# Four layer normalisations of a decoder kernel move from VectorE to ScalarE

## The chip, the cores and the metric

The kernel runs on one core of one Trainium2 chip. The metric is the device time of one launch in microseconds (us). The engines are TensorE (PE, with its weight loads shown apart as PEld), VectorE (DVE), ScalarE (ACT), GpSimd (POOL) and SyncE (SP), which issues the DMAs. All work is float32 but for a few constant matrices in bfloat16.

## The reference, cut to what matters

A two-layer post-norm decoder over 16 sequences of 128 tokens with 256 features. Each of the six sublayers ends in a plain normalisation (no gain, no bias):

```
x = norm(x + L0_attention(x))          # 16 heads, rotary, latent heads
x = norm(x + L0_cross(ctx, x))         # linear attention, own gain and bias inside
x = norm(x + L0_ffn(x))                # gate/up 704 wide, FP4 quantise-dequantise
x = norm(x + L1_attention(x))          # causal, with a moving-average part
x = norm(x + L1_cross(x, ctx))         # softmax attention, MLP 1024, own gains
x = norm(x + L1_ffn(x))                # FP6 quantise-dequantise
norm(y) = (y - mean(y)) / sqrt(var(y) + 1e-5)
```

## The kernel before, in words

One tile is one sequence: 128 tokens on the partitions, 256 features along them. Every engine runs a list of *stages* (`l0_out`, `f0_norm`, `x1_project`, ...) for 16 tiles. Tiles overlap: a new one starts every `START` step, and at any time work of five or six tiles is interleaved. The order of the stages is fixed per engine before the program is built: `in_order` (L132) sorts all (stage, tile) pairs by `START[tile] + SLOTS[engine][stage]`. So a slot number says only where a stage stands in its engine's own queue, and a stage that has to wait holds up all stages behind it on that engine. Data that belong to a tile lie in one of four buffers (`b = tile % 4`).

A sublayer ends like this. PE fills a PSUM bank; DVE adds the residual and stores `y_` (`residual`, L1014), and takes the moments with two instructions, BATCH_NORM_STATS2 and BATCH_NORM_AGGREGATE (`moments`, L1008: `stats`, then `mean_var`). POOL (`root`, L654) adds eps (`var_eps`) and raises to the power -0.5 (`rstd`). Then one engine has to make `x_ = (y_ - mean) * rstd`, 128x256. Before the change that is DVE for all six norms, in `center` (L1028): one TENSOR_SCALAR with two per-partition operands. Behind it wait, depending on the norm: a transpose on PE (`l1_turn_x`, `x0_turn_x`, `x1_turn_x`, L1579), a bias addition on POOL (`bias`, L642), a copy into `v_` on ACT (L861), a shifted copy by DMA (L595) or the store of the output (L622).

The names that the prediction uses, with their engines: `f0_down` (PE, then the residual on DVE) ends the first FFN; `f0_norm` its norm; `l1_turn_x` transposes the result on PE, ACT copies it out of PSUM into `xt_`, `l1_project` (PE) uses it, ACT evicts the projections (L867, L826) and makes the tanh keys `l1_ka` (L877), after which PE may start `l1_scores`. `l0_out`/`l0_norm` belong to the next tile's first attention, `l1_out`/`l1_norm` to the second attention, `f1_out`/`f1_norm` to the last sublayer. `f0_quant`, `f0_scale`, `f0_level` (DVE, L963 to L1169) quantise `x_`; POOL dequantises (L695) into `k_`, and PE transposes that in `f0_turn_x`. `x0_kv` is a projection on PE that needs the PSUM bank which the second group of exponentials (`l1_exp1`, ACT, L793) has to empty first; DVE gives the exponentials their offset in `low` (L1073) after a maximum (`peak`, L1068).

In steady state the queues around the norms read as follows (tile numbers relative, t the tile in its FFN):

```
DVE: f0_down(t) x1_norm(t-2) l0_back(t+1) f0_norm(t) f1_quant(t-2) l0_out(t+1) l0_norm(t+1) f1_scale(t-2) f1_level(t-2) x0_mix(t+1)
     ... l0_rope(t+2) f1_out(t-2) x0_norm(t+1) l1_back(t) f0_quant(t+1) f1_norm(t-2) l1_below(t) ... f0_scale(t+1) f0_level(t+1)
     ... l1_out(t) l0_peaks(t+2) l1_norm(t) f0_gate(t+1)
```

Of the kernel before, what the change touches and what calls it, by code (L numbers as in the profile page):

```python
# [87 lines left out]
        round_up2=75562, quant_down0=75911, l0_inv=76161, quant_down1=76187, l0_back=76275, round_down0=76280,  # L88
        l0_out=76309, round_down1=76325, l0_norm=76329, x0_mix=76505, quant_last=76662, round_last=76861,
        x0_attend=76881, x0_affine=77034, x0_norm=77121, f0_quant=77139, f0_scale=77266, f0_level=77351,  # L90
        wo_bias=77798, x1_mask=77829, f0_gate=78005, f0_gate2=78013, h_quant=78134, h_scale=78145,
        h_level=78303, f0_down=78591, f0_norm=78631, l1_project=78894, l1_scores=78980, l1_peaks=79103,
        l1_inv=79378, l1_back=79481, l1_below=79525, l1_ma=79530, l1_e=79578, x1_keys=79802, l1_ma_back=79805,
        l1_out=80217, l1_norm=80257, x1_peaks=80880, x1_scores=80895, x1_inv=81221, x1_back=81423, x1_out=81469,
        x1_affine1=81605, x1_down=83068, x1_affine2=83243, x1_norm=83307, f1_quant=83325, f1_scale=83416,
        f1_level=83442, f1_out=84147, f1_norm=84187),
    ACT=dict(turn_up0=0, l0_project=1626, l0_latent=3999, l0_exp1=4229, l0_exp0=4233, l0_exp2=4394,
        l0_exp3=4503, l0_copy1=4626, l0_copy0=4630, l0_v=4682, l0_spread=4956, turn_up1=5082, turn_up2=5686,
        x0_turn_x=5726, turn_down1=5851, x0_project=5954, turn_last=6404, f0_turn_x=6447, f0_up=6655,
        f0_turn_h=6992, f0_turn_h2=7020, l1_turn_x=7479, l1_project=7940, l1_ka=7952, l1_exp0=8164,  # L100
        l1_exp1=8328, l1_exp2=8384, l1_exp3=8475, l1_copy1=8538, l1_copy0=8563, l1_spread=8617, x1_turn_x=9277,
        x1_project=9300, x1_exp3=9425, x1_exp2=9492, x1_exp0=9773, x1_exp1=10062, x1_values=10195,
        x1_copy1=10362, x1_copy0=10374, x1_spread=10412, x1_turn_h=10960, x1_up=11025, x1_up2=11614,
        f1_turn_x=13200),
    POOL=dict(l0_rope=0, l0_mix=580, l0_out=1032, x0_project=1829, x0_attend=2066, x0_affine=2116,
        f0_level=2847, h_level=3026, f0_down=3230, l1_project=3318, l1_out=5276, x1_project=5286, x1_out=6525,
        x1_turn_h=7609, x1_down=7762, x1_affine2=7835, f1_level=8862, f1_turn_x=8864, f1_out=9844),
    SP=dict(l0_project=0, l1_turn_x=4652, x1_mask=4744, f0_down=4886, x1_scores=6996, f1_norm=9376),
)

MOVED = dict(
)
# [75 lines left out]
def plan_banks():  # L188
# [92 lines left out]
def decoder_kernel(nc, x, xT, ctxT, mask, cols, rows, const, bconst, c_attn, blocks, wqk, cproj,  # L281
                   x0_w, gate_up, down, l1_w, x1_w, w1, w2, fw, out):
    with ExitStack() as ctx:
# [444 lines left out]
        def _(act):  # L728
# [152 lines left out]
            def x1_up(stage, j):  # L881
# [33 lines left out]
        def _(dve):  # L915
# [313 lines left out]
            def x1_keys(i, b):  # L1229
# [19 lines left out]
                "x0_kv": x0_kv, "x0_mix": x0_mix, "x0_attend": residual("x0_attend", x_),  # L1249
                "l0_norm": center("l0_norm", "l0_out"), "x0_norm": center("x0_norm", "x0_affine"), "f0_norm": center("f0_norm", "f0_down"), "l1_norm": center("l1_norm", "l1_out"), "x1_norm": center("x1_norm", "x1_affine2"), "f1_norm": center("f1_norm", "f1_out"),  # L1250
                "x0_affine": affine_norm("x0_affine", "x0_attend", row["gamma"], lambda b: xb_[:, b, :],
# [585 lines left out]
```

## Time and profile before

| | us |
|---|---|
| median of 3 runs (lowest to highest) | 943.26 (942.33 to 944.02) |
| profiled execution, its own time | 942.33 |
| its span, first to last instruction | 940.5 |
| PE busy, DVE busy, ACT busy, POOL busy in the span | 832.2, 796.9, 605.5, 282.5 |

The 1.8 us between the span and the execution's time lie outside the instructions. A busy PE is not PE at its peak: the ends of matmuls are modelled, and overlapping ones are merged.

### The profile page before, as it was taken

What the parts mean: (1) busy time and instruction counts of PE and PEld (TensorE: products, weight loads), DVE (VectorE), ACT (ScalarE), POOL (GpSimd) and SP (SyncE); (2) the same over time, 40 slices, a digit from 0 to 9 for tenths busy, and PEclk for the clock granted to TensorE, in tenths of its full rate; (3) what the DMA queues carried; (4) which work ended last, traced back from release to release, by engine and by line L of the source; (5) the groups of instructions that cost most, each with busy time, mean ns of one, the idle gap of its engine ahead of it and who ended that gap; (6) DMA issues with size and microseconds to landing.
All of it is one profiled execution on the core that took longest, in us unless ns stands there. A gap on an engine that the chain in (4) does not pass through costs nothing.

```text
span 940.5 us, 29688 instructions
## 1 busy us (share of the span) xinstructions
PE 832.2 (88%) x11899; PEld 662.7 (70%) x11910; DVE 796.9 (85%) x1981; ACT 605.5 (64%) x2443; POOL 282.5 (30%) x490
## 2 busy tenths in 40 slices
PE   5576789999999999999999999999999999988864
PEld 4344556877778777777787787877787877766643
DVE  7896696989898999989898989899898989877553
ACT  2424558585768677685857686876858585746541
POOL 1121222233332333233333333332423333322121
PEclk8798999999999999999999999999999999999987
DMA  9300003000001000000000000000001000000000
GB/s 329 132 6 7 8 2 117 1 28 8 27 8 25 11 15 18 13 20 8 27 8 27 8 26 10 15 14 16 19 2 33 10 8 11 8 7 7 8 1 11
DMA packets 24442, 24.88 MB, mean 26 GB/s; under 512 B 2304, under 2 KB 22640, under 8 KB 24176
## 3 DMA queue, kind: packets, MB, share of 16 engines
q1 hardware_dynamic: 24304, 22.98, 7.5%
q8 instruction: 94, 1.54, 0.7%
q14 instruction: 44, 0.36, 0.1%
HBM read 18.80 MB, written 2.10 MB: 22 GB/s over the span
## 4 chain that ended last, share of the span: by engine, by line
PE 47%; DVE 34%; ACT 10%; issue 5%; POOL 3%; DMA 1%; DVEq 0%; SPq 0%; POOLq 0%
PE bank L1304 25%; PE s_tile L1304 16%; ACT prob L793 6%; DVE ma_ L1212 4%; DVE rope_ L1060 3%; DVE peak L1068 3%; DVE stats L1010 2%; PE bank L1425 2%; DVE x_ L1033 2%; PE bank L1514 2%; DVE y_ L1023 2%; ACT k_ L826 1%; DVE q_top L963 1%; POOL rstd L660 1%; DVE q_ L1168 1%
## 5 line engine op out<-in xcount | busy, mean ns | idle before, releaser
L793 ACT ACTIVATE prob<-s_tile,low 128x128 f32<-128x128 f32 x768 | 272.5, 408 | 23.8 <-DVE low L1073 23.7
L793 ACT ACTIVATION_READ_ACCUMULATOR prob<-s_tile,low 128x1 f32 x768 | 190.5, 248 | 0.0
L1068 DVE TENSOR_REDUCE peak<-s_tile 128x4 f32<-128x512 f32 x192 | 122.4, 679 | 12.4 <-PE s_tile L1304 12.4
L658 POOL TENSOR_TENSOR var_eps<-mean_var,rsq 128x1 f32<-128x1 f32 x144 | 32.4, 225 | 328.8 <-DVE mean_var L1012 328.8
L732 ACT ACTIVATE probT<-bank 128x512 f32<-128x512 f32 x192 | 99.5, 614 | 27.2 <-PE bank L1514 27.2
L660 POOL TENSOR_TENSOR rstd<-var_eps,rsq 128x1 f32<-128x1 f32 x144 | 84.0, 583 | 11.3
L732 ACT ACTIVATE xt_<-bank 128x256 f32<-128x256 f32 x64 | 24.5, 383 | 84.8 <-PE bank L1425 84.6
L1304 PE MATMUL bank<-w_gu,xt_ 128*128 128x352 f32 x256 | 78.4, 459 | 0.6 <-ACT xt_ L732 0.6
L1514 PEld LDWEIGHTS bank<-cst,prob 32*128 32x128 f32 x3072 | 54.0, 138 | 29.4 <-issue 13.1
L648 POOL TENSOR_TENSOR xb_<-x_,rowt 128x256 f32<-128x256 f32 x80 | 60.1, 755 | 26.1 <-DVE x_ L1033 26.1
L1514 PE MATMUL bank<-cst,prob 32*128 32x32 f32 x3072 | 59.7, 225 | 8.9 <-ACT prob L793 7.1
L1304 PEld LDWEIGHTS bank<-w_gu,xt_ 128*128 128x128 f32 x256 | 48.6, 190 | 25.3 <-ACT xt_ L732 0.8
L1010 DVE BATCH_NORM_STATS2 stats<-y_ 128x6 f32<-128x256 f32 x144 | 61.5, 427 | 5.0
L1304 PEld LDWEIGHTS bank<-xt_,w 128*128 128x128 f32 x512 | 60.7, 192 | 5.5 <-ACT xt_ L732 0.7
L1304 PE MATMUL bank<-xt_,w 128*128 128x128 f32 x512 | 63.8, 278 | 0.5 <-ACT xt_ L732 0.5
L1033 DVE TENSOR_SCALAR x_<-y_,mean_var,rstd 128x256 f32<-128x256 f32 x96 | 41.5, 433 | 23.0 <-POOL rstd L660 22.7
L695 POOL TENSOR_TENSOR k_<-q_,q_scale 128x256 f32<-128x256 f32 x32 | 19.8, 618 | 131.5 <-DVE q_ L1169 131.5
L695 POOL TENSOR_TENSOR ffn_<-ffn_,q_scale 128x704 f32<-128x704 f32 x16 | 22.2, 1387 | 118.3 <-DVE ffn_ L1169 118.3
L1304 PE MATMUL s_tile<-w_x,ct_ 128*128 128x256 f32 (+1 forms) x128 | 49.9, 514 | 7.7 <-ACT prob L793 7.6
L1304 PE MATMUL s_tile<-k_,q_ 32*128 32x128 f32 (+1 forms) x1280 | 55.1, 305 | 0.0
L1304 PE MATMUL bank<-probT,v_ 128*32 128x128 f32 x1536 | 53.6, 282 | 0.8 <-ACT xt_ L732 0.7
L1304 PE MATMUL s_tile<-xt_,w_l 128*128 128x128 f32 x384 | 47.1, 279 | 7.6 <-ACT xt_ L732 7.6
(204 smaller groups left out, 1950.0 us busy)
## 6 DMA issues: line engine op xcount, KB each, us to landing
xtin<-in_xT SPq DMA_DIRECT2D x16, 128.0 KB, 2.3
next_<-in_x SPq DMA_DIRECT2D x16, 128.0 KB, 6.3
ct_<-in_ctxT SPq DMA_DIRECT2D x16, 128.0 KB, 6.0
w<-in_w SPq DMA_DIRECT2D x2, 1024.0 KB, 8.1
out<-x_ SPq DMA_DIRECT2D x16, 128.0 KB, 1.7
next_<-x_ SPq DMA_DIRECT2D x16, 127.0 KB
rowt<-in_rows SPq DMA_DIRECT2D x1, 1664.0 KB, 9.1
w<-in_gate_up SPq DMA_DIRECT2D x2, 512.0 KB, 5.9
```

What stands on the lines that cost most here:

```text
L648: pool.tensor_tensor(xb_[:, b, :], source(b), term, ALU.add).then_inc(x_biased, 1)
L658: pool.tensor_tensor(var_eps[:, b:b + 1], mean_var[:, b, 1:2], rsq[:, 0:1], ALU.add) .then_inc(eps_in, 1)
L660: ins = pool.tensor_tensor(rstd[:, b:b + 1], var_eps[:, b:b + 1], rsq[:, 1:2], ALU.pow)
L695: pool.tensor_tensor(to(b).rearrange("p (a k) -> p a k", k=block), lev(b).rearrange("p (a k) -> p a k", k=block), long(q_scale[:, b % 2, a ...
L732: emptied(act.activation(dst, src, ACT.Copy), i, key)
L793: ins = act.activation(prob[:, r, c * P:(c + 1) * P], bank[r][:, c * P:(c + 1) * P], ACT.Exp, scale=SCALES[layer], bias=low[:, b, at0:at0 ...
L1010: dve.bn_stats(stats[:, b, :], y_[:, b, :]).then_inc(parted, 1)
L1033: dve.tensor_scalar(x_[:, b, :], y_[:, b, :], mean_var[:, b, 0:1], rstd[:, b:b + 1], ALU.subtract, ALU.mult).then_inc(centered, 1)
L1068: dve.tensor_reduce(peak[:, b, 4 * r:4 * r + 4], rows4(src[:, :]), AX_X, ALU.max)\
L1212: emptied(dve.tensor_tensor(rows4(ma_[:, r, :]), rows4(src[:, :]), wide(con["below"], 4), ALU.mult), i, ("l1_ma", b, S_BANKS[r]))
L1304: return pe.matmul(dst, lhsT, rhs, start=first, stop=last, **more)
L1514: ins = pe.transpose(bank[place(i, keys[g])[0]][:, at0:at0 + 32], prob[part, r, c * P:(c + 1) * P], ident[part, part])
```

## The change

Four of the six norms, `l0_norm`, `f0_norm`, `l1_norm` and `f1_norm`, leave DVE's queue and get a place in ACT's. `x0_norm` and `x1_norm` stay on DVE. ACT computes `x_ = rstd * y_ + shift` with one ACTIVATE (Identity, per-partition scale and bias). That needs `shift = -mean * rstd`, so for the four norms (`PLAIN`) POOL's `root` issues a third instruction, 128x1, after `rstd`, with a wait on its own semaphore between. The consumers wait on `x_new` (ACT) in place of `centered` (DVE). All other stages keep their slots on every engine, and `START` is unchanged. Two entries of `COVERED`, the list of PE's waits that are left out since an earlier wait implies them, change for `normed`: `x0_turn_x` of tile 0 has no wait any more, and for `x1_turn_x` the wait-free tiles go from 1 to 14 to 0 to 13.

```diff
     DVE=dict(...
-        l0_norm=76329, ... f0_norm=78631, ... l1_norm=80257, ... f1_norm=84187),
     ACT=dict(...
+        turn_up1=5082, l0_norm=5527, turn_up2=5686, ... f0_norm=7458, l1_turn_x=7479, ...
+        l1_spread=8617, l1_norm=9055, x1_turn_x=9277, ... f1_turn_x=13200, f1_norm=13344),
-MOVED = dict(
-)
-NEW_X = []
-CENTERED = ["l0_norm", "x0_norm", "f0_norm", "l1_norm", "x1_norm", "f1_norm"]
+NEW_X = ["l0_norm", "f0_norm", "l1_norm", "f1_norm"]
+CENTERED = ["x0_norm", "x1_norm"]
-PLAIN = []
+PLAIN = ["l0_out", "f0_down", "l1_out", "f1_out"]
-("x0_turn_x", "normed"): (1, 16)
+("x0_turn_x", "normed"): (0, 16)
-("x1_turn_x", "normed"): (1, 15)
+("x1_turn_x", "normed"): (0, 14)
+                "l0_norm": norm("l0_norm", "l0_out"),            # ACT's table
+                "f0_norm": norm("f0_norm", "f0_down"), "l1_norm": norm("l1_norm", "l1_out"),
+                "f1_norm": norm("f1_norm", "f1_out"),
-                "l0_norm": center(...), "x0_norm": center(...), "f0_norm": center(...), "l1_norm": center(...), ...
+                "x0_norm": center("x0_norm", "x0_affine"), "x1_norm": center("x1_norm", "x1_affine2"),
```

By the slot numbers the places in ACT's queue are: `f0_norm(t)` directly before `l1_turn_x(t)`; `l0_norm(t+1)` between `x1_values(t-1)` and `l1_project(t)`; `f1_norm(t-2)` between `l1_spread(t)` and `l0_project(t+3)`; `l1_norm(t)` between `f0_up(t+1)` and `l0_exp2(t+2)`.

## Rows read from the trace of the kernel before

**Rows 1.** The page's first part, engines over the whole span.
```profile
PE 832.2 (88%) x11899; PEld 662.7 (70%) x11910; DVE 796.9 (85%) x1981; ACT 605.5 (64%) x2443; POOL 282.5 (30%) x490
```
**Rows 2.** Busy time in stretches: span, its length, then each engine's busy us.
```profile
131.46:798.97 667.51, 635.47 (x9533) 512.63 (x9535) 601.01 (x1528) 479.87 (x1962) 222.35 (x381) 1.00 0.06 19
...
388.36:440.15 51.79, 49.25 (x739) 39.85 (x737) 46.81 (x120) 37.04 (x153) 17.46 (x30) 1.00 0.06 16
```
**Rows 3.** PE's waits from 131.46 to 798.97: total, times, longest (us).
```profile
PE s_tile L1304 <- ACT xt_ L877: 8.3, 13, 0.6
PE s_tile L1304 <- ACT xt_ L732: 6.2, 13, 0.5
...
PE s_tile L1304 <- ACT prob L793: 3.7, 12, 0.4
PE bank L1425 <- POOL k_ L695: 3.1, 12, 0.6
...
PE bank L1304 <- DVEq L1114: 0.9, 2, 0.5
```
**Rows 4.** DVE's and POOL's groups: count, busy, mean ns, idle before and releaser.
```profile
L1033 DVE TENSOR_SCALAR x_<-y_,mean_var,rstd 128x256 f32<-128x256 f32 x96 | 41.5, 433 | 23.0 <-POOL rstd L660 22.7
L658 POOL TENSOR_TENSOR var_eps<-mean_var,rsq 128x1 f32<-128x1 f32 x144 | 32.4, 225 | 328.8 <-DVE mean_var L1012 328.8
```
**Rows 5.** DVE in order of time (start, us): f0_norm, l0_norm, L1200, f1_norm and its successor.
```profile
402.02 0.41 DVE L1033 TENSOR_SCALAR x_<-y_,mean_var,rstd 128x256 f32<-128x256 f32 x1 [0.38 <-POOL rstd L660]
...
405.66 0.41 DVE L1033 TENSOR_SCALAR x_<-y_,mean_var,rstd 128x256 f32<-128x256 f32 x1 [0.94 <-POOL rstd L660]
...
408.83 0.86 DVE L1200 SCALAR_TENSOR_TENSOR q_<-q_ 128x256 f32<-128x256 f32 x1
...
426.12 0.41 DVE L1033 TENSOR_SCALAR x_<-y_,mean_var,rstd 128x256 f32<-128x256 f32 x1
426.44 2.47 DVE L1212 TENSOR_TENSOR ma_<-s_tile,cst 128x512 f32<-128x512 f32 x4
```
**Rows 6.** POOL in order of time: the power in f0_down's root.
```profile
401.44 0.55 POOL L660 TENSOR_TENSOR rstd<-var_eps,rsq 128x1 f32<-128x1 f32 x1
```
**Rows 7.** PE in order of time: l1_turn_x, f0_turn_x, x1_project.
```profile
402.93 0.38 PE L1425 MATMUL bank<-cst,x_ 128*128 128x128 f32 x2
...
432.49 0.44 PE L1425 MATMUL bank<-cst,k_ 128*128 128x128 f32 x2 [0.59 <-POOL k_ L695]
...
442.10 1.05 PE L1304 MATMUL bank<-xt_,w_x 128*128 128x128 f32 x8
```
**Rows 8.** ACT's groups: a copy, then ACTIVATEs with one and two per-partition operands.
```profile
L861 ACT ACTIVATE v_<-x_ 128x256 f32<-128x256 f32 x16 | 6.5, 408 | 0.0
...
L774 ACT ACTIVATE rope_<-bank,colt 128x128 f32<-128x128 f32 x64 | 18.3, 369 | 33.4 <-PE bank L1304 33.4
L826 ACT ACTIVATE k_<-s_tile,l1k_mb,colt 128x128 f32<-128x128 f32 x64 | 24.1, 457 | 4.3 <-PE s_tile L1304 4.3
```
**Rows 9.** ACT in order of time, at the four places where norms go in.
```profile
403.35 0.39 ACT L732 ACTIVATE xt_<-bank 128x256 f32<-128x256 f32 x1 [0.90 <-PE bank L1425]
...
406.77 1.51 ACT L826 ACTIVATE k_<-s_tile,l1k_mb,colt 128x128 f32<-128x128 f32 x4 [0.27 <-PE s_tile L1304]
...
427.41 1.14 ACT L887 ACTIVATE q_<-bank,colt 128x128 f32<-128x128 f32 x4 [2.95 <-PE bank L1304]
...
441.37 0.40 ACT L732 ACTIVATE xt_<-s_tile 128x256 f32<-128x256 f32 x1
```
**Rows 10.** The bank wait before x0_kv in an earlier tile.
```profile
261.59 1.95 PE L1304 MATMUL s_tile<-w_x,ct_ 128*128 128x512 f32 x4 [0.22 <-ACT prob L793]
```
**Rows 11.** DVE's L1200 late in the run, with POOL idle.
```profile
868.42 0.42 DVE L1200 SCALAR_TENSOR_TENSOR q_<-q_ 128x256 f32<-128x256 f32 x1 [1.85 <-ACT xt_ L877]
```
**Rows 12.** The last tile: PE's wait for f0_norm, then f1_norm.
```profile
862.47 0.44 PE L1425 MATMUL bank<-cst,x_ 128*128 128x128 f32 x2 [1.17 <-DVE x_ L1033]
...
937.87 0.41 DVE L1033 TENSOR_SCALAR x_<-y_,mean_var,rstd 128x256 f32<-128x256 f32 x1 [0.93 <-POOL rstd L660]
```

More of the change, by code:

```diff
@@ L88 @@
         round_up2=75562, quant_down0=75911, l0_inv=76161, quant_down1=76187, l0_back=76275, round_down0=76280,
[L89 to L96, printed above, removed]
-    ACT=dict(turn_up0=0, l0_project=1626, l0_latent=3999, l0_exp1=4229, l0_exp0=4233, l0_exp2=4394,
[L98 to L104, printed above, removed]
+        l0_out=76309, round_down1=76325, x0_mix=76505, quant_last=76662, round_last=76861, x0_attend=76881,
@@ new lines @@
+        x0_affine=77034, x0_norm=77121, f0_quant=77139, f0_scale=77266, f0_level=77351, wo_bias=77798,
+        x1_mask=77829, f0_gate=78005, f0_gate2=78013, h_quant=78134, h_scale=78145, h_level=78303,
+        f0_down=78591, l1_project=78894, l1_scores=78980, l1_peaks=79103, l1_inv=79378, l1_back=79481,
+        l1_below=79525, l1_ma=79530, l1_e=79578, x1_keys=79802, l1_ma_back=79805, l1_out=80217, x1_peaks=80880,
+        x1_scores=80895, x1_inv=81221, x1_back=81423, x1_out=81469, x1_affine1=81605, x1_down=83068,
@@ new lines @@
+        x1_affine2=83243, x1_norm=83307, f1_quant=83325, f1_scale=83416, f1_level=83442, f1_out=84147),
+    ACT=dict(turn_up0=0, l0_project=1626, l0_latent=3999, l0_exp1=4229, l0_exp0=4233, l0_exp2=4394,
+        l0_exp3=4503, l0_copy1=4626, l0_copy0=4630, l0_v=4682, l0_spread=4956, turn_up1=5082, l0_norm=5527,
+        turn_up2=5686, x0_turn_x=5726, turn_down1=5851, x0_project=5954, turn_last=6404, f0_turn_x=6447,
+        f0_up=6655, f0_turn_h=6992, f0_turn_h2=7020, f0_norm=7458, l1_turn_x=7479, l1_project=7940, l1_ka=7952,
+        l1_exp0=8164, l1_exp1=8328, l1_exp2=8384, l1_exp3=8475, l1_copy1=8538, l1_copy0=8563, l1_spread=8617,
+        l1_norm=9055, x1_turn_x=9277, x1_project=9300, x1_exp3=9425, x1_exp2=9492, x1_exp0=9773, x1_exp1=10062,
+        x1_values=10195, x1_copy1=10362, x1_copy0=10374, x1_spread=10412, x1_turn_h=10960, x1_up=11025,
+        x1_up2=11614, f1_turn_x=13200, f1_norm=13344),
@@ L1249, in _ @@
                 "x0_kv": x0_kv, "x0_mix": x0_mix, "x0_attend": residual("x0_attend", x_),
-                "l0_norm": center("l0_norm", "l0_out"), "x0_norm": center("x0_norm", "x0_affine"), "f0_norm": center("f0_norm", "f0_down"), "l1_norm": center("l1_norm", "l1_out"), "x1_norm": center("x1_norm", "x1_affine2"), "f1_norm": center("f1_norm", "f1_out"),
+                "x0_norm": center("x0_norm", "x0_affine"), "x1_norm": center("x1_norm", "x1_affine2"),
                 "x0_affine": affine_norm("x0_affine", "x0_attend", row["gamma"], lambda b: xb_[:, b, :],
```

4 rows, old and new, of the table COVERED are left out of this document.

## The prediction, made before the changed kernel was run

> **What bounds the kernel now.** I read the page's shares of busy time first, then the same in stretches, then PE's waits, and last the queues around the norms in order of time. Over the span PE is busy 88% and DVE 85% [rows 1], but that mixes a start and an end in which little overlaps. From 131 to 799 us thirteen tiles pass at 51.3 us each (667.5 / 13), PE is busy 635.5 of 667.5 us (95%) and DVE 601.0 (90%); in one tile of 51.8 us PE works 49.3, DVE 46.8, ACT 37.0 [rows 2]. So PE is the bound, and it has 32.0 us of waits in that stretch, 2.5 per tile. A change that relieves DVE can give back only those of PE's waits that DVE causes. PE's list of waits sorts them [rows 3]. 8.3 us wait for ACT's tanh keys (l1_ka), 6.2 us for ACT's copy of the transposed x_: each is a round trip PE, ACT, PE of thirteen tiles with nothing of DVE in it. Three kinds do depend on DVE: 3.7 us for the exponentials, whose offsets DVE makes, 3.1 us for POOL's k_ (the dequantised x of f0, behind f0_level), 0.9 us for the semaphore that DVE raises behind l1_e. Together 7.7 us: the ceiling of what a faster DVE is worth in the steady stretch.
>
> **What leaves DVE.** 64 of the 96 instructions of one group, 433 ns on average [rows 4]: 27.7 us of busy time. Some idle time goes with them, since DVE stands still until POOL's power is ready: 0.38 us before f0_norm and 0.94 us before l0_norm in the tile shown [rows 5]. Per tile that is about 4 x 0.43 + 1.3 = 3.0 us. Very little of it reaches PE. The first 2.1 us (f0_norm and l0_norm with their waits) lie ahead of L1200, which starts at 408.83 us, when ACT has just finished the tanh keys that it reads (in three of the thirteen tiles it waited some 0.6 us for them). ACT gets these keys from PE, so DVE would arrive early and wait there. Behind that point only f1_norm remains, at 426.12 us, with its successor at 426.44 [rows 5]: about 0.33 us of queue time. And it lies on the way from x0_kv to f0_level.
>
> **Term 1, the wait for k_.** PE starts f0_turn_x at 432.49 after a wait of 0.59 [rows 7]; over twelve such waits it is 3.1 us, mostly 0.24 each. DVE is 0.33 us earlier without f1_norm, which covers all but the longest. I take all of it: -3.1 us. Bounds: 0, if DVE waits elsewhere in the chain, to -3.1.
>
> **Term 2, the exponentials.** 3.7 us in twelve waits. In some tiles it is 0.41, in others 0.22 [rows 10]; the short ones are tiles in which DVE already waited for PE's scores, so 0.22 is what the round trip costs with an early DVE. 3.7 - 12 x 0.23 = 0.9: -0.9 us, bounds 0 and -3.7. **Term 3, l1_e's semaphore.** 0.9 us in two waits of about 0.48 [rows 3]; DVE 0.33 earlier on each: -0.6 us, bounds 0 and -0.9.
>
> **Term 4, f0_norm's new path.** Now: power on POOL from 401.44, 0.55 long, ends 401.99 [rows 6]; DVE's norm 402.02 to 402.43 [rows 5]; PE takes x_ at 402.93 [rows 7], straight behind other work, so the slack is 0.50 less a hand-over of 0.05. After: a hand-over of 0.07 on POOL, the shift, then an ACTIVATE. No row shows a 128x1 TENSOR_SCALAR on POOL; its neighbours in root are 0.22 (eps, mean) [rows 4] and 0.55 (power) [rows 6], and I take 0.20, near the first and as simple. No row shows the ACTIVATE either: the same size copied is 408 ns, and the step from one per-partition operand to two on 128x128 is 457 - 369 = 88 ns [rows 8]; two of them give 0.58. From below it is 0.41, from above 0.41 + 2 x 0.17 = 0.75. x_ is then ready at 401.99 + 0.07 + 0.20 + 0.05 + 0.58 = 402.89 instead of 402.43, and PE needs 0.05 more: 402.94 against 402.93. ACT is free by then: the exponentials of the tile before end at about 402.3, and it idles 0.90 us before the copy of l1_turn_x [rows 9]. In three of thirteen tiles PE already waited for this norm. I take 0.05 per tile: +0.65 us. Bounds per tile: 0, to 402.0 + 0.07 + 0.55 + 0.05 + 0.75 + 0.05 = 403.46, that is +0.53.
>
> **Term 5, the rest of ACT's queue.** An ACTIVATE of this kind keeps the queue about 0.46 us (copies of this size follow each other at 0.28, plus twice 0.09). l0_norm goes in just ahead of l1_project; ACT waits 0.27 there before k_ and 0.17 before q_ [rows 9], and DVE's l0_out finishes in time for it: nothing. f1_norm goes ahead of l0_project(10), whose eviction ran at 423.3; POOL's power for f1_out ends at 425.5, so l0_project moves back by some 3 us, to about 426.3 to 427.3. Queued behind it is x1_up, which started at 427.41 after 2.95 idle us waiting for PE [rows 9]: just covered. PE needs the evicted bank again for x1_keys at 428.3: covered by 1 us. Without that idle time the 3 us would stand on PE's path. l1_norm goes into a stretch where ACT has no gap, ahead of l0_exp2, x1_up2 and the copy for x1_project. That copy ends at 441.77, PE starts x1_project at 442.10 [rows 7, 9], a slack of 0.3. ACT is 0.46 later and, since DVE's l0 offsets come some 0.1 to 0.3 earlier, it costs PE 0 to 0.2: I take 0.1 per tile, +1.3 us. POOL has 16 x 4 more small instructions, but it is 30% busy; SP's transfers wait for the same norms and had 25 us of room (next_ is read in l1_e).
>
> **Term 6, the end.** In the last tile nothing overlaps. The path runs through f0_norm (PE waits 1.17 us for it at 862.47) and f1_norm (937.87, the last instruction before the store) [rows 12]. Each becomes 0.07 + 0.20 + 0.17 = 0.45 us longer: +0.9. l1_norm of that tile has 0.8 us of slack. The start stays as it is: l0_norm of tile 0 gets 0.1 later, DVE's rounding of weights 0.3 earlier.
>
> **Sum.** -3.1 - 0.9 - 0.6 + 0.65 + 1.3 + 0.9 = -1.75 us. The profiled execution took 942.33 (span 940.5 and 1.8 outside): 940.6. That execution was the fastest of the three shown; their median, 943.26, is 0.9 above it, and the same sum from there gives 941.5. I forecast 940.6, for what DVE gains without a wait of PE pointing to it can only lower it. Its own range is 938 to 943.
>
> **A rule against it.** L1200 took 0.86 us while POOL was adding biases and 0.42 when POOL was idle [rows 5, 11]: the two engines hinder each other. The Trainium skill ("SBUF — State Buffer", section "SBUF: two separate sides") says why: VectorE and GpSimd share one pair of ports under an exclusive lock, taken for a whole instruction, and the loser waits. The trace agrees with the doubling. By that rule the four shifts per tile are four more chances to meet a DVE instruction, in f0's case the quantiser's reduction, which now comes right behind l0_back; a shift that waits for it would come out near the upper bound of term 4, and the sum would be the slow rival's. Against that it takes 64 DVE instructions away from the power.
>
> **Rivals.** (a) *All of DVE's share comes back.* Terms 1 to 3 at their ends, -7.7, terms 4 and 5 nil, the end +0.9: 942.3 - 6.8 = 935.5. For it: DVE has only 10% of idle time, and POOL's bias additions move away from L1200. Against it: the exponentials' wait has a floor of 0.22 in tiles with an early DVE. (b) *Nothing arrives.* DVE's 3 us turn into waits of DVE, and what terms 1 to 3 give, 4.6, terms 4 to 6 take at a little over their middle: 942 to 943. This is also the case in which the load moves but the bound doesn't. For it: PE's largest waits do not name DVE. (c) *ACT becomes late, slower.* Place: f0_norm between POOL's power and l1_turn_x. It decides when shift and ACTIVATE together take over 0.8 us, where 0.78 is estimated. With a shift as long as the power (0.55) x_ is 0.36 late, 13 x 0.36 = +4.7; the copy behind l1_norm uses no earlier offsets, +0.18 x 13 = +2.3; the end 2 x 0.8 = +1.6; terms 1 to 3 still give 4.6: 942.3 + 4.0 = 946.3. For it: slack is zero by my own sum. Against it: no 128x1 instruction but the power is above 0.3.
>
> **How the numbers follow.** Forecast 0.40, (a) 0.20, (b) 0.22, (c) 0.18. A measurement of this kernel tells a difference of about 0.2%, 1.9 us, from none. Faster by more: (a) and 0.7 of the forecast, 0.48. Within: most of (b) and 0.3 of the forecast, 0.32. Slower: (c) and a rest of (b), 0.20. The range, 935 to 947, holds (a) and (c) at their price and leaves out the bounds taken all at once (term 4 at +0.53 per tile would be 6.9 us alone).
>
> **What would show it.** Right: DVE busy lower by about 27 us and ACT higher by 29 to 37 (64 x 0.46 to 0.58); PE's waits for POOL's k_ gone from the steady stretch, those for the exponentials near 0.22 each, those for the tanh keys and for xt_ unchanged at 0.64 and 0.47; longer DVE waits before L1200; a tile of about 51.2 us. Wrong: PE waiting for ACT's x_ before l1_turn_x in every tile (then (c)), shifts over 0.3 us, x1_up on ACT starting late behind f1_norm and l0_project, or PE's tanh wait shrinking, which would mean that DVE was on that path after all.

## The result and the profile after

The changed kernel takes 949.82 us (median of four runs, 949.14 to 950.41), the kernel before 943.64 on the same chip (four runs, 942.33 to 944.39): a ratio of 1.0066, 95% interval 1.0049 to 1.0084. It is slower by 6.2 us; I had forecast 1.75 us less. The profiled execution took 949.62 us, its span is 947.7 (940.5 before).

The first part of the page after, then busy time in stretches (as [rows 2]; the column behind the engines is the granted clock of TensorE, 1.00 for 2.4 GHz and 0.50 for 1.2): the thirteen steady tiles, and the one that answers to 388.36:440.15 before. (That one is not typical: before, it was one of two long tiles, 51.79 and 51.84 us against 50.93 to 51.44 for the other eleven. The median of the thirteen tiles is 51.35 before and 51.46 after.)

```profile
PE 842.9 (89%) x11910; PEld 664.1 (70%) x11910; DVE 766.7 (81%) x1917; ACT 635.5 (67%) x2507; POOL 301.6 (32%) x554
```
```profile
134.64:803.54 668.90, 641.53 (x9534) 512.38 (x9535) 576.58 (x1476) 502.61 (x2010) 237.63 (x432) 1.00 0.06 19
392.10:443.55 51.45, 49.60 (x738) 39.75 (x737) 44.55 (x116) 38.77 (x158) 18.54 (x34) 1.00 0.05 16
```

The load moved as planned: DVE has 30.2 us less than in [rows 1], ACT 30.0 more, POOL 19.1 more. Of DVE's 30.2, the 64 norms are 26.9 (41.5 - 14.6); another 5.8 is an instruction that did not move, L1200 (L1196 after), whose sixteen take 6.8 us instead of 12.6, 0.42 each as in [rows 11]. The thirteen tiles did not get shorter: 668.9 us against 667.5 [rows 2], though DVE works 24.4 us less in them. PE's waits in that stretch (as [rows 3]):

```profile
PE s_tile L1300 <- ACT xt_ L873: 8.3, 13, 0.6
PE s_tile L1300 <- ACT xt_ L728: 6.2, 13, 0.5
PE bank L1300 <- DVE y_ L1019: 5.5, 13, 0.6
PE s_tile L1300 <- ACT prob L789: 2.6, 12, 0.2
PE bank L1421 <- POOL k_ L691: 0.5, 2, 0.2
```

So the waits that terms 1 to 3 were about did go: k_ from 3.1 to 0.5, the exponentials from 3.7 to 2.6, the DVEq wait from 0.9 to nothing. And the tile is longer all the same. The groups show what the new steps cost, and, in the last row of each kernel, where DVE's freed time went (after | before):

```profile
L837 ACT ACTIVATE x_<-y_,shift,rstd 128x256 f32<-128x256 f32 x64 | 39.2, 612 | 61.8 <-POOL shift L662 61.8
L662 POOL TENSOR_SCALAR shift<-mean_var,rstd 128x1 f32<-128x1 f32 x64 | 19.2, 300 | 6.3
L1029 DVE TENSOR_SCALAR x_<-y_,mean_var,rstd 128x256 f32<-128x256 f32 x32 | 14.6, 457 | 0.9 <-POOL rstd L656 0.9
L1123 DVE TENSOR_TENSOR cross_<-s_tile,cst 128x256 f32<-128x256 f32 x16 | 6.8, 424 | 22.6 <-PE s_tile L1300 22.6
```
```profile
L1127 DVE TENSOR_TENSOR cross_<-s_tile,cst 128x256 f32<-128x256 f32 x16 | 6.7, 418 | 3.3 <-PE s_tile L1304 3.3
```

In x0_mix, DVE stood still 3.3 us for PE before and stands still 22.6 us after: 19.3 us of what DVE gained is waiting for a PE that comes no earlier. The wait ahead of L1200 (L1196 after), which the prediction named, grew too, from 5.6 to 11.6 us.

The span's 7.2 us can be split at the same anchor, the start of x1_turn_x of tiles 0 and 13 on PE: *start* is what lies ahead of tile 0's, *drain* what lies behind tile 13's. The table has the same for every run below (us; the warm stages are explained in the third set). It holds one profiled execution of each kernel, which is not always near its median. The steady column repeats well: 667.3 to 667.5 for the three runs with all norms on DVE and no shift, 663.3 to 663.9 for the five with f1_norm alone. The start column does not: in before, f1 only, f1 in tiles 0-12, all in tiles 1-12 and the f1 run with warm stages in the drain alone, nothing ahead of the first anchor differs, and the start is 131.5 to 133.3. The first matmul alone, which waits for a transfer, comes between 8.1 and 9.5 us in these traces.

| | start | 13 steady tiles | drain | span |
|---|---|---|---|---|
| before | 131.5 | 667.5 | 141.5 | 940.5 |
| after | 134.6 | 668.9 | 144.2 | 947.7 |
| l1 only | 132.3 | 670.6 | 144.6 | 947.6 |
| f1 only | 132.2 | 663.6 | 145.9 | 941.7 |
| f0 only | 132.1 | 668.1 | 144.1 | 944.3 |
| l0 only | 134.8 | 676.0 | 144.1 | 954.9 |
| l0, f0 | 131.0 | 667.6 | 144.1 | 942.7 |
| l0, f0, f1 | 135.4 | 663.9 | 146.0 | 945.3 |
| shift only | 132.5 | 675.9 | 147.3 | 955.7 |
| f1, tiles 0-12 | 133.3 | 663.5 | 145.6 | 942.4 |
| all, tiles 1-12 | 132.4 | 668.7 | 143.5 | 944.5 |
| before + first warm set | 130.0 | 667.3 | 141.6 | 938.9 |
| f1, tiles 0-12 + first warm set | 131.5 | 663.9 | 142.7 | 938.1 |
| after + first warm set | 132.9 | 667.9 | 144.3 | 945.1 |
| f1, tiles 0-12 + warm, drain only | 131.5 | 663.3 | 142.8 | 937.6 |
| f1, tiles 0-12 + ten warm stages | 130.3 | 663.3 | 141.0 | 934.6 |
| before + the same ten | 132.8 | 667.4 | 143.0 | 943.2 |

Start and drain together hold 5.8 of the 7.2. Part of it is TensorE's clock. Stretches of before, then of after:

```profile
88.00:92.00 4.00, 4.00 (x14) 3.39 (x15) 0.80 (x1) 1.26 (x3) 0.66 (x1) 0.56 0.03 8
92.00:96.00 4.00, 3.84 (x48) 2.97 (x48) 1.46 (x4) 0.38 (x1) 0.74 (x2) 1.00 0.10 29
884.00:888.00 4.00, 3.46 (x51) 2.98 (x50) 2.44 (x6) 1.14 (x4) 0.00 (x0) 1.00 0.02 6
```
```profile
88.00:92.00 4.00, 2.83 (x10) 2.37 (x10) 2.15 (x1) 0.60 (x1) 2.01 (x2) 0.50 0.00 0
92.00:96.00 4.00, 4.00 (x13) 3.29 (x13) 0.00 (x0) 0.66 (x2) 0.00 (x0) 0.59 0.13 37
884.00:888.00 4.00, 3.95 (x48) 2.92 (x50) 1.16 (x4) 1.87 (x5) 1.19 (x4) 0.60 0.00 0
```

After, the clock is low until about 95.3 us instead of 91.5, and low again from 883.8 to 887.2, behind a 0.74 us wait; before, it stayed at 1.00 behind the same wait of 0.75. It is also low from 136 to 140 us, inside the first steady tile, where before it is not. In the order in which the time is lost: PE's x0_turn_x(0) comes at 58.73 instead of 57.40, of which 0.4 is already there in the first transfers; the longer low stretch at 92 to 96 costs 1.2 us; in the drain x_ of f0_norm(15) reaches PE after 1.74 us instead of 1.17 [rows 12]; the low stretch at 884 costs 1.3; the copy ahead of x1_project(15) 0.2 (PE waits 0.65 for it instead of 0.47); and f1_norm(15) some 0.5. The low stretch at 136 is in the steady column: in the run of this kernel with warm stages, which lacks it, the first tile takes 50.6 us instead of 51.6 and the other twelve agree within 0.1 us each. Here is the first of these waits, then the one for f0_norm(15):

```profile
58.73 0.44 PE L1421 MATMUL bank<-cst,x_ 128*128 128x128 f32 x2 [2.79 <-ACT w_gu L728]
867.54 0.44 PE L1421 MATMUL bank<-cst,x_ 128*128 128x128 f32 x2 [1.74 <-ACT x_ L837]
```

The first names ACT's w_gu, not x_: l0_norm(0) stands in ACT's queue in front of `turn_up2`, an eviction of weights which used to be done by then. PE's wait there is 2.30 to 2.79 us in the five traces with l0_norm(0) on ACT and 1.13 to 1.87 in all others, so this part of the start's loss, 0.9 us here, repeats.

### The profile page after: what moved, and what is told of

It is laid out like the page before. It is cut to its first block, busy times and chain, and to the rows that moved or that the text cites. A ratio compares the mean times of both kernels' runs of the same rounds, so it can differ in the third digit from the quotient of the medians.

```text
span 947.7 us, 29761 instructions
## 1 busy us (share of the span) xinstructions
PE 842.9 (89%) x11910; PEld 664.1 (70%) x11910; DVE 766.7 (81%) x1917; ACT 635.5 (67%) x2507; POOL 301.6 (32%) x554
## 4 chain that ended last, share of the span: by engine, by line
PE 46%; ACT 26%; DVE 21%; issue 4%; POOL 2%; DMA 1%; DVEq 0%; SPq 0%; POOLq 0%
PE bank L1300 23%; PE s_tile L1300 17%; ACT prob L789 15%; DVE peak L1064 4%; PE bank L1510 3%; ACT k_ L822 3%; PE bank L1421 2%; DVE ma_ L1208 2%; DVE rope_ L1056 2%; ACT x_ L837 2%; ACT k_ L883 1%; DVE stats L1006 1%; ACT ffn_ L845 1%; ACT xt_ L873 1%; DMA q_<-in_c_attn 1%
## 5 line engine op out<-in xcount | busy, mean ns | idle before, releaser
L837 ACT ACTIVATE x_<-y_,shift,rstd 128x256 f32<-128x256 f32 x64 | 39.2, 612 | 61.8 <-POOL shift L662 61.8
L644 POOL TENSOR_TENSOR xb_<-x_,rowt 128x256 f32<-128x256 f32 x80 | 58.0, 730 | 36.9 <-ACT x_ L837 36.0
L1300 PEld LDWEIGHTS s_tile<-xt_,w_l 128*128 128x128 f32 x384 | 44.1, 192 | 11.4 <-ACT xt_ L728 11.4
```

The lines of the kernel that those rows point to most:

```text
L644: pool.tensor_tensor(xb_[:, b, :], source(b), term, ALU.add).then_inc(x_biased, 1)
L837: act.activation(x_[:, b, :], y_[:, b, :], ACT.Identity, scale=rstd[:, b:b + 1], bias=shift[:, b:b + 1]).then_inc(x_new, 1)
L1300: return pe.matmul(dst, lhsT, rhs, start=first, stop=last, **more)
```

## Experiments, first set: one norm at a time

Each kernel moves one norm, with its place on ACT and its shift on POOL exactly as in the change; the other three stay on DVE. For example:

```diff
-NEW_X = []
+NEW_X = ["l1_norm"]
-PLAIN = []
+PLAIN = ["l1_out"]
```

**l1_norm alone.** 

> Only l1_norm moves to ACT, with its shift on POOL; the other three stay on DVE. Theory A (one place on ACT does the harm: l1_norm has no gap there and holds back the copy that x1_project waits for): x1_project starts about 0.4 us later after x1_turn_x in every steady tile, the tile grows from 51.35 to about 51.7 us, the whole by 4 to 5 us (about 947.5). Theory B (all four insertions cost alike, by ACT's load): about +1.6 us. Theory C (the loss is the TensorE clock's, which happened to stay low longer in the start and fell once in the drain): the time follows the clock stretches, with steady tiles unchanged.

Measured: 949.0 us (948.37 to 950.19, four runs), ratio 1.0060 [1.0041, 1.0079]. The steady stretch:

```profile
132.34:802.97 670.63, 638.88 (x9534) 511.80 (x9535) 597.34 (x1514) 485.38 (x1972) 226.48 (x394) 1.00 0.07 19
```

+3.1 us over before, 0.24 per tile on average, with nothing gained. Tile by tile it is steadier than that: the first got 0.4 us shorter, the other twelve 3.5 longer together, 0.29 each.

**f1_norm alone** (`NEW_X = ["f1_norm"]`, `PLAIN = ["f1_out"]`). 

> Only f1_norm moves to ACT. Theory A: this is the one with a gain, since it alone lies between x0_kv and f0_level on DVE: the wait for k_ (0.24 per tile) goes, the tile falls to about 51.0 us, 13 x 0.33 = -4.3, the end +0.5: about 940. Theory B: +1.6 us. Theory C: set by the clock stretches, tiles unchanged.

Measured: 942.89 us (939.51 to 944.74, ten runs), ratio 0.9991 [0.9975, 1.0007]. The steady stretch is 3.9 us shorter than before:

```profile
132.20:795.84 663.64, 635.00 (x9534) 512.74 (x9535) 598.05 (x1516) 485.16 (x1974) 225.72 (x393) 1.00 0.06 19
```

The waits for k_ and for l1_e's semaphore are gone from its list, the exponentials' stays at 3.7: terms 1 and 3 are f1_norm's. The drain, though, gives back 4.3 us.

**f0_norm alone** (`NEW_X = ["f0_norm"]`, `PLAIN = ["f0_down"]`). 

> Only f0_norm moves to ACT. Theory A: l1_turn_x starts 0.08 to 0.13 us later per tile (+1.0 to 1.7), +0.25 at the first tile, +0.57 at the last: +2 to +2.5, about 946. DVE's 0.7 us per tile would come back nowhere. Theory B: +1.6. Theory C: set by the clock stretches.

Measured: 946.3 us (944.96 to 947.03, six runs), ratio 1.0027 [1.0015, 1.0038]. Here the exponentials' wait falls, so term 2 is f0_norm's:

```profile
PE s_tile L1305 <- ACT prob L793: 2.7, 12, 0.2
```

With that 1.0 us gained the steady stretch is still 0.6 longer. Counted from x1_turn_x of the same tile, l1_turn_x starts 0.01 to 0.11 us later, 1.0 us over the thirteen tiles, and in every tile PE's weight load now waits for x_ (before: 0.9 us in three):

```profile
PEld bank L1426 <- ACT x_ L841: 4.3, 13, 0.4
```

**l0_norm alone** (`NEW_X = ["l0_norm"]`, `PLAIN = ["l0_out"]`). 

> Only l0_norm moves to ACT. Theory A: steady tiles lose nothing or gain up to 0.1 us (DVE's 1.3 us go, but DVE then waits for the tanh keys), the first tile costs 0.9 us since l0_norm stands in ACT's queue ahead of the eviction of transposed weights (turn_up2) that PE waits for: 0 to +1 us, about 944. Theory B: +1.6. Theory C: set by the clock stretches.

Measured: 953.37 us (951.49 to 956.71, four runs), ratio 1.0110 [1.0081, 1.0138], more than the whole change. No theory had expected it. ACT's queue and PE's wait in tile 3, then PE's waits of the stretch, then two windows of that tile:

```profile
307.33 0.60 ACT L841 ACTIVATE x_<-y_,shift,rstd 128x256 f32<-128x256 f32 x1 [0.61 <-POOL shift L666]
310.50 0.44 PE L1305 MATMUL s_tile<-below_tab,bcst 32*32 32x512 bf16 x16 [1.19 <-ACT xt_ L877]
```
```profile
PE s_tile L1305 <- ACT xt_ L877: 13.6, 13, 1.5
```
```profile
308.00:312.00 4.00, 2.81 (x94) 2.27 (x96) 1.94 (x5) 4.00 (x12) 1.76 (x3) 0.88 0.09 26
312.00:316.00 4.00, 4.00 (x51) 2.77 (x48) 2.23 (x6) 2.36 (x11) 0.00 (x0) 0.69 0.00 0
```

The ACTIVATE stands 0.61 us waiting for its shift, with l1_project's evictions and the tanh keys queued behind it. PE's wait for the keys rises from 0.64 to 1.19 (8.3 to 13.6 in the stretch), and behind that longer wait the clock fell in three of the thirteen tiles (311, 468 and 676 us), which took 53.2 to 53.5 us instead of 51.4 to 51.8. The execution in this trace is the slowest of the four (956.71): its span is 14.4 us longer than before, the medians differ by 10.1, so its steady stretch (+8.5 us) may overstate the usual loss.

## Second set: interaction, place in time, and the shift

**f1_norm on ACT in tiles 0 to 12 only.**

```diff
+ON_ACT = {"f1_norm": (0, 13)}      # ACT's order has these tiles, DVE's the others; no shift for those
```

> Only f1_norm goes to ScalarE, and only for tiles 0 to 12; tiles 13 to 15 keep it on VectorE, with no shift on POOL, so that start and drain are the queues of the kernel before. With f1_norm alone in all tiles the thirteen steady tiles took 663.6 us instead of 667.5 (the wait for k_ and l1_e's semaphore gone), but its run gave most of that back in the drain: the granted clock fell there at 860 and 878 us behind the very waits (1.18 and 0.71 us) behind which it had stayed high before. Theory A (the steady gain is real, the drain is a draw of the clock plus the two norms at the end): steady stretch 663.6 again, the runs spread over 938.4 to 942, median about 939.5 to 940.5. Theory C (the clock takes it back whatever is done in the drain): steady 663.6, but a median of 942 to 943. Theory B (f1_norm's gain was a draw of that one profile): steady 667 and 943.

Measured: 943.49 us (941.29 to 944.49, ten runs), ratio 1.0009 [0.9999, 1.0018]. The steady gain is there again (663.5), so B falls; A's median isn't: theory C's figure came out, or slightly more (942 to 943 expected). From x1_turn_x(14) to l1_project(15) PE's rows are those of before moved by 2.44 us, with the same waits of 1.17 and 0.47 us ahead of l1_turn_x(15) and l1_project(15). Before, then this kernel:

```profile
862.00:866.00 4.00, 3.06 (x25) 2.83 (x26) 3.69 (x12) 2.90 (x13) 0.93 (x2) 1.00 0.04 12
```
```profile
860.00:864.00 4.00, 3.50 (x19) 3.26 (x20) 3.69 (x11) 2.36 (x11) 1.34 (x2) 0.70 0.04 13
```

Around l1_turn_x(15) work and waits are the same, and the clock stayed up in one kernel and fell in the other. l1_project took 4.57 us instead of 2.94.

**All four norms on ACT, in tiles 1 to 12 only** (`ON_ACT` with (1, 13) for each). 

> All four norms on ScalarE, but only for tiles 1 to 12; in tiles 0 and 13 to 15 they stay on VectorE without a shift, so that the start and the last three tiles are the queues of the kernel before. Theory A (the loss of the whole change, 6.6 us, is 1.4 us in the steady tiles and some 5 us in the start and the drain, by later norms on a bare path and by the clock that falls with them): steady stretch about 669, start and drain as before, 943.3 + 1.4 = 944.7, at most 946. Theory B (the steady tiles cost more than one profile showed): 949 again. Theory C (clock): the steady stretch holds, but the clock falls in the drain at places of its own, 944 to 948 with a wide spread.

Measured: 946.17 us (944.39 to 947.01, five runs), ratio 1.0036 [1.0022, 1.0051]. The steady stretch is 668.7, as in the change; against the kernel before in its own set (943.01) the loss is 3.2 us instead of 6.2, so giving start and drain their old queues brings back 3.0. That is less than A's 5: its trace has falls of the clock at 870 and 881 us that the one of before lacks, so part of what C says holds too.

**l0_norm and f0_norm.** (`NEW_X = ["l0_norm", "f0_norm"]`) 

> l0_norm and f0_norm on ScalarE in all tiles, l1_norm and f1_norm on VectorE. With l0_norm alone its ACTIVATE stood 0.6 us waiting for the shift in front of q_ and k_ of l1_project, PE's wait for the tanh keys rose from 8.3 to 13.6 us over thirteen tiles, and three tiles lost another 1.7 us each to a fall of the clock behind that wait. Theory A (l0_norm is late only because f0_norm, which stands before l0_out in VectorE's queue, still holds that queue; in the whole change it costs nothing there): tanh wait back at 8.3 to 8.5, no clock fall in the steady tiles, steady stretch 667 to 669, time 946 to 949. Rival (the two costs add, l0_norm's place is bad by itself): tanh wait 13 or more, steady stretch 676, time 955 or more.

Measured: 945.49 us (944.47 to 950.98, eight runs), ratio 1.0034 [1.0013, 1.0055]. Theory A holds: PE's wait for the tanh keys is back at its old value, and the steady stretch at 667.6.

```profile
130.99:798.58 667.59, 637.02 (x9533) 512.43 (x9535) 583.74 (x1502) 491.64 (x1988) 230.58 (x407) 1.00 0.06 19
```

f0_norm stands ahead of l0_out in DVE's queue, and waits there for POOL. With it gone, l0_out ends early enough for l0_norm to cost ACT nothing. So l0_norm's move is harmful alone (+8.5 us in the steady tiles of its trace) and free there in company.

**The shift alone.** All norms stay on DVE; POOL computes the four shifts, unused, and the norms wait for them.

```diff
-PLAIN = []
+PLAIN = ["l0_out", "f0_down", "l1_out", "f1_out"]
```

> All norms stay on VectorE; only POOL's third instruction of root (shift = -mean * rstd) is added for the four norms, which then wait for it; ScalarE is as before. Theory A (the shift costs its 0.30 us where a path is bare and nothing by contention): POOL busy +19, steady stretch 667.5 to 670 (f0_norm's slack takes most of 0.35 us), the two norms at the end +0.7, time 943.5 to 946. Rival (VectorE and POOL hinder each other, each shift delays VectorE or is delayed): shifts of 0.5 us or more, DVE's instructions beside them longer, steady stretch over 671, time 947 or more. A result under 943 would mean that delays in VectorE's queue cost PE nothing.

Measured: 955.26 us (952.99 and 957.52), ratio 1.0135 [1.0104, 1.0166]. There are only two runs, 4.5 us apart, and the trace is of the slower. The rival's number, but not its mechanism: the shift takes 0.26 to 0.27 us in 63 of 64 cases. What grows is DVE's standing still ahead of its norms, 35.1 us instead of 23.0 [rows 4]. Its group of norms, its steady stretch, and the new first entry of PE's waits:

```profile
L1034 DVE TENSOR_SCALAR x_<-y_,mean_var,rstd 128x256 f32<-128x256 f32 x96 | 42.2, 439 | 35.1 <-POOL shift L666 34.2 <-POOL rstd L660 0.9
```
```profile
132.53:808.39 675.86, 639.29 (x9534) 513.14 (x9536) 601.87 (x1528) 479.09 (x1962) 236.05 (x432) 1.00 0.06 19
```
```profile
PE s_tile L1305 <- DVE cross_ L1128: 8.8, 9, 1.2
```

DVE's queue thus has nearly no slack towards later and little worth towards earlier: in the thirteen tiles, 52 norms taken away bought 4.6 us of PE's waits, and with 12 us of added waiting over the run the stretch is 8.4 us longer (some 1.2 of it by a fall of the clock at 673 us). How much of the rest goes by DVE's queue, and how much by x_ itself coming later to PE, this run doesn't separate.

## Third set: TensorE's clock by itself, and a better version

A *warm* stage is the kernel's own filler: four bfloat16 matmuls of 512 columns into a free bank, used by nobody. The kernel has 14. These runs place more where the traces show PE idle ahead of a fall.

```diff
+warm14=89650, warm15=89230, warm16..20=53440..53444    # f1_out(13); l1_scores(15); five before f0_turn_h(0)
-warm8=88803
+warm8=88900                                            # before l1_turn_x(15)
```

**In the kernel before.** 

> The kernel before with matmuls of no use (the kernel's own warm stages, four bfloat16 matmuls of 512 columns each) where PE stands idle ahead of a fall of the granted clock: five more between l0_mix3(1) and f0_turn_h(0), where PE waits 6 us for POOL's ffn_ and the clock stays at 0.50 from 84.8 to 91.7 us; one between x1_mix3(14) and l1_scores(15), one before f1_out(13), and warm8 moved from before x1_values(14) to before l1_turn_x(15). Theory D (TensorE's clock is a cost of its own, and the kernel's PE work right behind an idle stretch pays it): granted clock 1.00 from 84 to 92 us, the 3.9 us of work there take 2 us less, l0_norm(0) and all behind it come 1 to 2 us earlier, 943.0 - 1.5 = 941.5 (940.5 to 942.5); the drain of this kernel rarely had falls at 860 to 884, so little there. Rival E (the start is bound by VectorE's or GpSimd's work, not by PE's): the clock is up but the time stays at 943.

Measured: 943.89 us (940.49 to 946.85, eleven runs), ratio 1.0005 [0.9991, 1.0019]: no gain in the median. The profiled run (940.65) has no low stretch at 84 to 92 and a start shorter by 1.4 us, as D says; three runs were at 940.5 to 940.8 with a mean clock of 0.978, the others mostly at 943.3 to 944.5 with 0.971 to 0.975. Where those fell has no trace. Inconclusive.

**With f1_norm on ACT in tiles 0 to 12.** 

> f1_norm on ScalarE for tiles 0 to 12 (as in the earlier run of it, 943.5 us, with a steady stretch of 663.5 and falls of the clock at 861, 868 and 878 us), with the same warm stages as the run above. Theory D: no low stretch at 84 to 92 and none at 858 to 884; start -1.5, drain -3 to -4, which are the 3.9 us that the steady tiles gained and the drain gave back: 938 to 939.5, faster than both kernels. Rival E: 943. Rival F (the falls in the drain only move to the next wait, at 886 or 900): start gain alone, 941.5 to 942.5.

Measured: 939.42 us (938.39 to 939.9, five runs), ratio 0.9960 [0.9948, 0.9973]. Faster than both kernels. The falls at 86, 868 and 878 are gone, those at 102 (behind a wait of 1.75) and 133 (1.17) are new, and the one at 860 stayed: warm8 moved past x1_values, but PE's wait of 1.17 behind it was as long as before.

**In the changed kernel.** 

> The changed kernel (all four norms on ScalarE in all tiles) with the same warm stages. Its clock was at 0.50 from 85 to 95.8 us, from 136.4 to 139.7 and from 883 to 887. Theory D: 949.8 less 2.5 at the start and 1.3 in the drain: 945 to 947, which would leave of the loss of 6.6 the 1.4 of the steady tiles, the two norms on the bare path at the end and a rest. Rival E: 949 to 950, the loss is in queues and paths alone.

Measured: 947.28 us (944.93 to 949.13, nine runs), ratio 1.0044 [1.0032, 1.0056]. The low stretches at 85 to 95, 136 and 883 are gone, and 2.5 us with them. Just above D's range; and 4.4 us of the loss are not the clock of these places. Its trace also has something that D left out: from 902 to 915 the clock is low without a break, where the changed kernel had two short falls, and the stretch behind x1_turn_x(15) takes 51.2 us instead of 49.7. So part of what the filled waits gave was lost again further on, and 2.5 us is not an upper bound on the clock's share.

**f1_norm, warm stages of the drain alone.** 

> f1_norm on ScalarE for tiles 0 to 12, with the warm stages of the drain alone (warm8 moved before l1_turn_x(15), one before l1_scores(15), one before f1_out(13)); the start is as before. Theory D: steady stretch 663.5, no low stretch at 858 to 884, 943.5 - 3 = 940.5 (939.5 to 941.5). Rival F (the falls move on, or the warm stages delay PE by what they save): 942.5 to 944.

Measured: 940.16 us (938.78 to 942.79, eleven runs), ratio 0.9974 [0.9963, 0.9984]. D's time came out: against the same kernel without them (943.49, in the set before) two added stages and a moved one, which compute nothing, bring 3.3 us. Its stretches only in part: the falls at 868 and 878 are gone, but the one behind l1_turn_x(15) is still there (859 to 863, l1_project 4.57 us), where D had expected none.

**The change without l1_norm** (`NEW_X = ["l0_norm", "f0_norm", "f1_norm"]`, all tiles). 

> The change without l1_norm: l0_norm, f0_norm and f1_norm on ScalarE in all tiles, l1_norm on VectorE. Theory A (l1_norm's ACTIVATE, 0.6 us in the stretch in which ScalarE has no gap, is the step that turns the steady tiles from a gain to a loss: 0.24 us per tile alone): steady stretch 668.9 - 3.1 = 665.8 or a little less, and the start and the drain keep most of their loss: 949.8 - 3 to 4 = 946 to 947. Theory B (the four norms cost alike): steady 668, 948.5. Theory C (the clock decides, the norms hardly): 949 with the falls in the same places.

Measured: 945.32 us (940.47 to 948.08, ten runs), ratio 1.0023 [1.0006, 1.0041], and the steady stretch

```profile
135.35:799.26 663.91, 638.18 (x9534) 513.08 (x9535) 580.42 (x1490) 496.66 (x2000) 233.42 (x419) 1.00 0.06 19
```

Five us less than in the change, more than A's 3.1: l1_norm turns the steady tiles from -3.6 to +1.4. Both traces have a fall at 136 to 140 in their first tile; in the twelve behind it the difference is 4.9 us, 0.41 each. Start and drain keep their loss, as A said; in this trace, which is 1.8 us over the median, it is even larger than the change's.

**f1_norm and ten warm stages, one at each wait of note.**

```diff
+warm14=89650, warm15=89230, warm16=88900, warm17..21=53440..53444, warm22=54000, warm23=55470   # warm8 stays
```

> f1_norm on ScalarE for tiles 0 to 12, with ten more warm stages: five in the 6 us wait before f0_turn_h(0), one before l1_scores(0) (wait of 1.75 us at 101), one before x1_project(0) (1.17 at 133), and in the drain one before l1_turn_x(15) (1.17 at 858; warm8, moved there earlier from before x1_values(14), had left this wait as long), one before l1_scores(15) and one before f1_out(13). The earlier run with warm stages (939.4) still had low stretches at 102 to 109, 133 to 136 and 860 to 863. Theory D (each of them costs 1 to 1.7 us and goes when the wait is filled): none of the three left, steady stretch 663.5, 936 to 937.5. Rival F (they move to the next wait or the warm stages delay PE by as much): 939 to 940.

Measured: 936.38 us (936.05 to 936.99, six runs), ratio 0.9928 [0.9909, 0.9948]. The three places that had been low, 84, 102 to 136 and 860, are at 1.00; two of them:

```profile
84.00:88.00 4.00, 2.90 (x14) 1.11 (x12) 3.85 (x6) 0.61 (x2) 0.97 (x1) 1.00 0.01 4
860.00:864.00 4.00, 3.89 (x106) 2.72 (x104) 1.86 (x5) 3.73 (x12) 0.61 (x1) 1.00 0.09 26
```

**The kernel before with the same ten.** 

> The kernel before with the same ten warm stages, all norms on VectorE. Theory D: the start gives 1.5 to 2.5 us, the drain little (its falls at 860 to 884 were rare): 940.5 to 941.5, and the difference to the run above, 3.9 us of the steady tiles, is what f1_norm on ScalarE is worth. If f1_norm's gain were only a matter of the clock, both would be equal.

Measured: 942.65 us (941.17 to 945.01, twelve runs), ratio 0.9996 [0.9981, 1.0011]. So the warm stages alone are worth nothing measurable there, and the pair differs by 6.3 us. The steady tiles explain 4.1 of it (667.4 against 663.3). The rest lies in start and drain, and the traces can't divide it well, since the one of this kernel is its slowest execution (945.01): it has a fall at 73 to 76 us, ahead of the first added stage, and one at 879 to 882, the other has neither. Why is open.

## Why the prediction was wrong, point by point

**What bounds the kernel, and terms 1 to 3** (-3.1, -0.9, -0.6; together -4.6). Right in mechanism and about right in size: 2.6, 1.1 and 0.9 of PE's waits went, and f1_norm alone made the steady stretch 3.9 us shorter. (L1200 had waited for the tanh keys in four of the thirteen tiles, not in three; nothing hangs on it.) Of the place where DVE would wait instead I had named the smaller one: L1200 has 6.0 us more, x0_mix 19.3.

**Term 4, f0_norm** (+0.65). Right in mechanism, somewhat under-sized: the shift takes 0.27 there (0.20 taken), the ACTIVATE 0.60 (0.58), and l1_turn_x starts 1.0 us later over the thirteen tiles with f0_norm alone. The Trainium skill ("ScalarE: Activation LUTs", section "What ACT_TABLE_LOAD costs") gives an ACTIVATE's time by its size and its per-partition operands; worked out for this one that is an estimate of 0.59 us, and the trace agrees with a mean of 0.612.

**Term 5, the step that failed in the steady tiles.** "It costs PE 0 to 0.2: I take 0.1 per tile, +1.3 us" was for l1_norm; it measures +0.24 per tile alone (3.1 us) and +0.38 in company (668.9 - 663.9 = 5.0 us). It shows best in one tile. ACT after, then PE after; both answer to [rows 7, 9]:

```profile
440.99 0.65 ACT L837 ACTIVATE x_<-y_,shift,rstd 128x256 f32<-128x256 f32 x1
445.21 0.52 ACT L728 ACTIVATE xt_<-s_tile 128x256 f32<-128x256 f32 x1
```
```profile
445.79 1.16 PE L1300 MATMUL bank<-xt_,w_x 128*128 128x128 f32 x8
```

From x1_turn_x's start, ACT's copy comes at 445.21 - 443.55 = 1.66 us, where it was 441.37 - 440.15 = 1.22, and takes 0.52 instead of 0.40: it ends 0.56 later. PE's x1_project comes at 2.24, where it was 1.95 [rows 7, 9]. So the slack was there, and used up: 0.33 from the copy's end to x1_project before, 0.06 after, and 0.56 - 0.27 is the 0.29 that PE lost. What was mis-sized is the delay. I had taken 0.46 less 0.1 to 0.3 for l0's exponentials starting earlier; but they follow f0_up on ACT without a gap in both kernels, so earlier offsets move nothing, and nearly the whole length of the ACTIVATE arrives, with a longer copy on top. Without l1_norm (the run above) x1_project is back at 1.94 to 1.95 in the twelve tiles behind the first. Another 0.10 per tile, which the prediction had nothing for, is lost between x1_project and the transposes of ffn_ that follow it: 5.04 us from start to start instead of 4.94, in the change and with l1_norm alone, and 4.94 again without it. PE's list names no wait ahead of x1_project in this tile, before or after: the modelled ends of the matmuls cover nearly all of the gap. That is why the list of waits got shorter while the tile got longer. For l0_norm, "nothing" was right, but only because f0_norm moves too; f1_norm's push of l0_project stayed covered.

**Term 6, the other step that failed** (+0.9, "the start stays as it is"). The start lost 3.2 us and the drain 2.6. The end's two norms were sized about right (0.57 and about 0.5, for 0.45 each). What was not in the sum at all: l0_norm(0) in front of an eviction of weights that PE waits for (0.9 us), and TensorE's clock (1.2 us in the start, 1.0 in the first steady tile, 1.3 in the drain, in the one execution traced). Filling waits brought 2.5 us back in the changed kernel.

**The sum.** Forecast for the span: -2.65 in the steady tiles, 0 in the start, +0.9 in the drain. Measured: +1.4, +3.2, +2.6. So of the 9.0 us between the two, 4.0 lie in the steady tiles, 3.2 in the start and 1.7 in the drain. In the steady tiles the moves nearly add: f1_norm alone -3.9, l0_norm with f0_norm +0.1, the three together -3.6; l1_norm on top of them +5.0. Had term 5 been 5.0 and term 4 1.0, the forecast would have been -4.6 + 1.0 + 5.0 + 0.9 = +2.3, slower, and the rest is the start's and the clock's.

**The rule against it.** The Trainium skill ("SBUF — State Buffer", section "SBUF: two separate sides") has VectorE and GpSimd lock a shared port pair for a whole instruction, on VectorE's side for its two-port modes, or when it reads two inputs from SBUF while GpSimd reads SBUF. The trace agrees in a small way: 50 of the 64 shifts take 0.26 or 0.27 us, but 13, l0_out's one in thirteen tiles, take 0.41 or 0.42, and lie beside a 128x256 TENSOR_TENSOR of DVE with both inputs in SBUF that takes 0.42. That norm was not on the path. f0's shift, for which the prediction had feared the quantiser, lies beside instructions with one tensor input and stayed at 0.27. The rule did not decide the outcome. The other way round DVE gained: L1200 takes 0.86 to 0.95 us in twelve tiles before and in the same tiles with l1_norm or f1_norm alone, and 0.42 or 0.43 in all tiles of the four runs that have l0_norm on ACT in every tile and no added stages. Like the rest of DVE's freed time, that went into waiting.

**Rivals.** (c) had the sign, and a part of the price: its copy behind l1_norm was put at 0.18 per tile. Its condition was met too, if barely: shift and ACTIVATE take 0.27 + 0.60 = 0.87 us together, over its 0.8, and PE's weight load waits for x_ ahead of l1_turn_x in every tile (4.3 us, the sign named for it). But its main place was wrong: f0_norm ahead of l1_turn_x costs 1.0 us in the steady tiles, not 4.7.

## What to carry to other kernels

Moving work off a busy engine is worth only the waits of the bounding engine that name it, and each piece should be moved and timed alone and then in company: in the steady tiles here one of four moves paid (-3.9 us), one was free only with another, and one (l1_norm) cost more than the first gave. An instruction put into a stretch in which an engine has no gap delays that stretch's next hand-over by nearly its whole length; only the slack measured at that hand-over (here 0.27 us) comes off, and nothing for inputs that arrive earlier. A change that shortens or shifts an engine's queue also moves the idle stretches of TensorE, so look at the granted clock of start and drain in both traces, and re-place the filler work.

## What the hardware showed that I had not expected

TensorE's clock fell to 0.50 for 3.4 us or more at a time (883.8 to 887.2 in the changed kernel) behind waits of PE as short as 0.7 to 1.2 us, even amid tiles in which PE is over 90% busy (311 us, with l0_norm alone), and each such short fall cost 1.0 to 1.8 us. It isn't decided by the wait alone: the same 1.17 us wait, with the same matmuls just before it, left the clock up in one kernel and not in another whose same work ran 2.4 us earlier. What makes the difference is not settled by these runs. The Trainium skill ("TensorE: Matmul & The Clock Gate", section "What's actually happening") says that the gate's watch on the engine runs free and isn't set back by the start of a kernel, so that a change of clock varies from run to run; these runs fit that, in that the difference found was the place in time, but none of them tests it. Filling waits of PE at ten places with matmuls that nobody uses made one kernel 6.4 us faster (943.49 to 936.38, in different sets; 0.5 over and 6.0 under the kernel before, which was at 943.01 and 942.35 in them) and another not at all.
